# Two conditional residual MLPs in sequence: opening DMAs reordered over two queues, slot tables packed, adapter picks shared between engines

## The reference

```
w1, w2 = W1[language], W2[language]              # 10 languages, 128x32 and 32x128
h = relu(x @ w1 + b1[language])
y = x + h @ w2 + b2[language]
x = x + layernorm(y) * gamma[language] + beta[language]

s0, s1, s2 = relu(x @ share_wi[m]) @ share_wo[m]  # 128 -> 512 -> 128, all sequences
out_a, out_b = the same with experts type and type + 1 of four
e = wa * out_a + wb * out_b                       # weights from softmax(gate_vecs / 0.1)
g = softmax(relu(concat(e[0], s0[0], s1[0], s2[0]) @ gate_w1) @ gate_w2)   # first token
x = x + g0 * e + g1 * s0 + g2 * s1 + g3 * s2
```

## Time and profile before

| | us |
|---|---|
| median of 3 runs | 85.97 (85.92 to 86.11) |
| the profiled execution | 85.84 |
| its span | 83.9 |

### The profile page before, as it was taken

One profiled execution on the slowest core, in us unless ns is written; L12 is line 12 of the kernel. 1 busy time (PEld: TensorE's weight loads), 2 busy tenths in 40 slices (PEclk: granted clock), 3 DMA queues, 4 the chain that ended last, 5 costly groups with the idle time before them and its releaser, 6 DMA issues.

```text
span 83.9 us, 1644 instructions
## 1 busy us (share of the span) xinstructions
PE 77.1 (92%) x458; PEld 64.7 (77%) x458; DVE 56.7 (68%) x161; ACT 54.3 (65%) x136; POOL 44.2 (53%) x92
## 2 busy tenths in 40 slices
PE   4999985999999999999999999999999999999720
PEld 1355645867878899988999988888999998999510
DVE  4357696899659665375445664579749996689930
ACT  0726876595997989997899964745545654566110
POOL 4882452999999877178975400000006981069400
PEclk9999999999999999999999999999999999999999
DMA  0784776899997491000000000000000000210021
GB/s 3 174 174 85 226 208 177 253 299 342 335 286 241 131 324 63 0 0 0 8 0 0 0 0 0 0 4 0 0 8 0 0 0 0 62 62 8 0 71 58
DMA packets 12151, 7.56 MB, mean 90 GB/s; under 512 B 2501, under 2 KB 10969, under 8 KB 12141
## 3 DMA queue, kind: packets, MB, share of 16 engines
q1 hardware_dynamic: 11984, 7.39, 30.7%
q0 software_dynamic: 96, 0.05, 0.6%
q10 hardware_dynamic: 60, 0.01, 0.1%
HBM read 5.87 MB, written 0.52 MB: 76 GB/s over the span
## 4 chain that ended last, share of the span: by engine, by line
PE 75%; DVE 7%; POOL 7%; ACT 4%; issue 3%; DVEq 0%; ACTq 0%
PE bank L1052 10%; PE bank L1003 10%; PE bank L1049 9%; PE bank L1050 9%; PE bank L1004 9%; PE bank L1005 9%; PE bank L1083 4%; POOL prod L530 3%; PE bank L1077 2%; PE bank L1057 2%; PE bank L969 2%; POOL prod L532 2%; PE bank L959 1%; DVE gv L761 1%; PE bank L943 1%
## 5 line engine op out<-in xcount | busy, mean ns | idle before, releaser
L816 DVE SCALAR_TENSOR_TENSOR hl<-bank,hh 128x256 fp32r<-128x256 f32 (+2 forms) x60 | 31.3, 526 | 16.1 <-ACT hh L608 15.7
L608 ACT ACTIVATE hh<-bank 128x256 fp32r<-128x256 f32 (+2 forms) x60 | 28.2, 470 | 14.5 <-PE bank L1005 12.4
L486 POOL TENSOR_TENSOR wl<-w_raw,wh 128x512 fp32r<-128x512 f32 x18 | 23.1, 1290 | 8.5 <-ACT wh L601 8.4
L1052 PE MATMUL bank<-hl,wh 128*128 128x256 f32 (+2 forms) x60 | 20.3, 338 | 0.1
L1049 PE MATMUL bank<-hh,wh 128*128 128x256 f32 (+2 forms) x60 | 19.7, 329 | 0.0
L1050 PE MATMUL bank<-hh,wl 128*128 128x256 f32 (+2 forms) x60 | 19.6, 326 | 0.0
L1052 PEld LDWEIGHTS bank<-hl,wh 128*128 128x128 f32 x60 | 11.3, 189 | 2.1 <-DVE hl L816 1.2
L1049 PEld LDWEIGHTS bank<-hh,wh 128*128 128x128 f32 x60 | 11.4, 190 | 0.9
L1050 PEld LDWEIGHTS bank<-hh,wl 128*128 128x128 f32 x60 | 11.4, 189 | 0.7
L601 ACT ACTIVATE wh<-w_raw 128x512 fp32r<-128x512 f32 x18 | 11.3, 629 | 0.0
L1003 PE MATMUL bank<-x1hl,wh 128*128 128x256 f32 (+1 forms) x34 | 11.2, 329 | 0.0
(11 more groups left out here) (117 smaller groups left out, 111.3 us busy)
## 6 DMA issues: line engine op xcount, KB each, us to landing
w_raw<-in_L_cond_expert_wi_dram SPq DMA_DIRECT2D x6, 256.0 KB, 4.3
w_raw<-in_L_cond_expert_wo_dram SPq DMA_DIRECT2D x6, 256.0 KB, 4.4
w_raw<-in_L_cond_share_wi_dram SPq DMA_DIRECT2D x3, 256.0 KB, 2.9
w_raw<-in_L_cond_share_wo_dram SPq DMA_DIRECT2D x3, 256.0 KB, 3.1
x_in<-in_x_dram SPq DMA_DIRECT2D x2, 256.0 KB, 3.4
xs<-x1hl SPq DMA_DIRECT2D x4, 128.0 KB, 4.5
x1hl<-xs SPq DMA_DIRECT2D x4, 128.0 KB, 2.5
out_dram<-o_sb SPq DMA_DIRECT2D x4, 128.0 KB, 1.9
```

Source lines behind the costliest of these rows:

```text
L486: nc.gpsimd.tensor_tensor(wl[:, k, w, :], w_raw[:, k, buf(w), :], wh[:, k, w, :].bitcast(f32), ALU.subtract).then_inc(s_wl[w], 1)
L608: nc.scalar.activation(packed(hh[:, u % NBUF, :], r), packed(h_ps[u % NBUF][:, :], r), ACT.Relu).then_inc(s_hh, 1)
L816: nc.vector.scalar_tensor_tensor(out=packed(hl[:, u % NBUF, :], r), in0=packed(h_ps[u % NBUF][:, :], r), scalar=0.0, in1=packed(hh[:, u % ...
L1052: nc.tensor.matmul(dst, wh[:, 1, w, chunk], lo, start=False, stop=(c == FC - 1)).then_inc(s_mm2, 1)
```

## The change

- SP's first DMAs are x half 0, W1 and x half 1; `language`, which was ahead of them, and `type`, which was fourth, are issued by ACT: `language` ahead of gamma, beta and b1, `type` behind them.
- WARM goes from 8 to 7.
- Three slot starts or experts are packed in one integer: two tables with 17 memsets in place of six with 24. DVE, not POOL, multiplies, sums and converts. Engines load two integers, and `load_packed` takes three values out of each by shifts and masks.
- POOL takes the four picks of W1 for half 1 in place of ACT.
- On ACT, the copy of xT for half 1 goes ahead of the first root, `weights_high(0, 0)` ahead of the second, and `weights_high(0, 1)` ahead of both x1_high.
- On PE, `transpose_x(1)` goes ahead of `adapter_out(0)`; `load_starts` goes from the end of the opening to a place ahead of `adapter_in(1)`; `adapter_out` is called for each pair, and pairs 2 and 3, which were inside `opening_products`, stand on either side of `transpose_z(1)`.

```diff
-    NQ, NK = 2 * len(SIZES), B + 1
-    STEPS = {0: {3: 3, 4: 3, 5: -3, 6: 3}, 1: {0: 1, 2: 1, 3: -2, 4: 4, 5: 1, 6: -2, 7: 1}, 2: {0: 4, 4: -4},
-             3: {1: -2, 3: 2, 5: -2, 6: 2, 8: -2}, 4: {3: -2, 4: 2, 6: -2}, 5: {4: -2}}
+    NQ, NK = 2, B + 1
+    BITS = (3, 2)
+    STARTS = ({3: 3, 4: 3, 5: -3, 6: 3}, {0: 1, 2: 1, 3: -2, 4: 4, 5: 1, 6: -2, 7: 1}, {0: 4, 4: -4})
+    EXPERTS = ({1: -2, 3: 2, 5: -2, 6: 2, 8: -2}, {3: -2, 4: 2, 6: -2}, {4: -2})
+    STEPS = [{k: sum(at.get(k, 0) << bits * i for i, at in enumerate(what)) for k in range(NK)}
+             for bits, what in zip(BITS, (STARTS, EXPERTS))]
-    WARM = 8
+    WARM = 7
...
+        def load_packed(engine, name, q, tops):
+
+            engine.wait_ge(s_tab, 1)
+            top = (1 << len(SIZES) * BITS[q]) - 1
+            both = loaded(engine, name, tab_i[0:1, B + 2 * q:B + 2 * q + 2], [top] * 2)
+            values = []
+            for (par, i), t in zip(SLOT_OF, tops):
+                reg = engine.alloc_register(f"{name}_{par}{i}")
+                engine.reg_mov(reg, (both[par] >> BITS[q] * i) & ((1 << BITS[q]) - 1))
+                values.append(engine.snap(reg, min_val=0, max_val=t))
+            return values
...
         def _(sp):
-            sp.dma_start(lang_p[:, :], on_all(language)).then_inc(s_lang, 16)
             sp.dma_start(x_in[:, half(0), :], x[half(0), :, :].rearrange("b s d -> s b d")).then_inc(s_x[0], 16)
             sp.dma_start(W1t[:, :, :], W1.rearrange("l d a -> d l a")).then_inc(s_w1, 16)
-            sp.dma_start(kind_p[:, :], on_all(kind)).then_inc(s_kind, 16)
...
-            window_tables()
+            pick_adapters()
+            pool.wait_ge(s_tab, 1)
...
+            act.dma_start(lang_p[:, :], on_all(language)).then_inc(s_lang, 16)
             act.dma_start(par_l[:, 0, :], gamma).then_inc(s_gb, 16)
             act.dma_start(par_l[:, 1, :], beta).then_inc(s_gb, 16)
             act.dma_start(b1_l[:, :], b1).then_inc(s_b1in, 16)
+            act.dma_start(kind_p[:, :], on_all(kind)).then_inc(s_kind, 16)
...
-            pick_adapters(0)
+            pick_adapters()
             add_beta((0, 1))
             adapter_relu(0)
             add_beta((2, 3))
-            pick_adapters(1)
-            standard_deviation(0)
             act.wait_ge(s_xt, 2)
             nc.scalar.activation(xT[:, cols(1)], xt_ps[1][:, :], ACT.Copy).then_inc(s_xtc[1], 1)
+            standard_deviation(0)
+            weights_high(0, 0)
             standard_deviation(1)
-            weights_high(0, 0)
             adapter_relu(1)
+            weights_high(0, 1)
             x1_high(0)
             x1_high(1)
-            weights_high(0, 1)
...
                 stt(key[:, :], kind_f[:, :], float(B), no_b, ALU.mult, ALU.add)
                 tt(sq[:, :, :], across(key[:, :], B), down(key[:, :], B), ALU.is_lt)
-                nc.vector.tensor_reduce(tab[:, 0:B], sq[:, :, :], AX.X, ALU.add).then_inc(s_sorted, 1)
+                total(tab[:, 0:B], sq[:, :, :])
+                dve.wait_ge(s_steps, STEP_COUNT)
+                tt(taken[:, :, :, :], steps[:, :, :, :], reached[:, :, :].unsqueeze(2).to_broadcast([P, 2, NQ, NK]),
+                   ALU.mult)
+                total(tab[:, B:].rearrange("p (q s) -> p s q", s=2), taken[:, :, :, :])
+                nc.vector.tensor_copy(tab_i[:, :], tab[:, :]).then_inc(s_tab, 1)
...
                     with_high(0)
                     if n == 0:
                         with_high(1)
-                        adapter_out(1)
                         pe.wait_ge(s_x1l, 1)
...
             residual(0)
             adapter_in(0)
+            transpose_x(1)
+            adapter_out(0)
             residual(1)
-            adapter_out(0)
-            transpose_x(1)
+            adapter_out(1)
+            starts = load_starts(pe)
+            adapter_in(1)
             residual(2)
-            adapter_in(1)
             transpose_z(0)
             residual(3)
+            adapter_out(2)
             transpose_z(1)
-            starts = load_starts(pe)
+            adapter_out(3)
             opening_products()
```

More of the change, by code:

```diff
@@ L87, in conditional_residual_mlps @@
     BUFS = SH + RING
-    NQ, NK = 2 * len(SIZES), B + 1
-    STEPS = {0: {3: 3, 4: 3, 5: -3, 6: 3}, 1: {0: 1, 2: 1, 3: -2, 4: 4, 5: 1, 6: -2, 7: 1}, 2: {0: 4, 4: -4},
-             3: {1: -2, 3: 2, 5: -2, 6: 2, 8: -2}, 4: {3: -2, 4: 2, 6: -2}, 5: {4: -2}}
+    NQ, NK = 2, B + 1
[4 more added lines that the diff above has]
+             for bits, what in zip(BITS, (STARTS, EXPERTS))]
+    STEP_COUNT = sum(1 for at in STEPS for k, v in at.items() if v and k) + 2 * NQ
+    FIRST_EXPERT = sum(1 << BITS[1] * i for i in range(len(SIZES)))
     UNITS = [(r, c) for r in range(len(RUNS)) for c in range(FC)]
@@ L266, in conditional_residual_mlps @@
         s_steps = sem("s_steps")
-        s_sorted = sem("s_sorted")
         s_tab = sem("s_tab")
@@ L310, in buf @@
             return w if w < SH else SH + (w - SH) % RING
-        def place(k, what):
-            return B + SLOTS * what + k
         def size(k):
@@ L347, in loaded @@
             return [engine.snap(reg, min_val=0, max_val=top) for reg, top in zip(regs, tops)]
+        def load_packed(engine, name, q, tops):
[8 more added lines that the diff above has]
+            return values
         def load_starts(engine):
-            engine.wait_ge(s_tab, 1)
-            return loaded(engine, "start", tab_i[0:1, place(0, 0):place(SLOTS, 0)], [B - size(k) for k in range(SLOTS)])
+            return load_packed(engine, "start", 0, [B - size(k) for k in range(SLOTS)])
         def load_adapters(engine, langs, h):
@@ L392, in _ @@
             load_wo(sp, 1, share_wo[1, :, :])
-            sp.wait_ge(s_tab, 1)
-            experts = loaded(sp, "expert", tab_i[0:1, place(0, 1):place(SLOTS, 1)], [E - 1] * SLOTS)
+            experts = load_packed(sp, "expert", 1, [E - 1] * SLOTS)
             for k in range(RING):
@@ L454, in _, with pick_adapters @@
             link(nc.gpsimd.memset(steps[:, :, :, :], 0.0))
-            for q, at in STEPS.items():
+            for q, at in enumerate(STEPS):
                 for k, v in at.items():
[L457 to L474, removed]
+                    for par in range(2):
+                        value = v + (q * FIRST_EXPERT * (2 + par) if k == 0 else 0)
+                        if value and (par == 0 or k == 0):
+                            pars = slice(par, par + 1) if k == 0 else slice(0, 2)
+                            nc.gpsimd.memset(steps[:, pars, q, k:k + 1], float(value)).then_inc(s_steps, 1)
+            def pick_adapters():
+                pool.wait_ge(s_lang, 16)
+                langs = loaded(pool, "lang", lang_p[0:1, HB:B], [L - 1] * HB)
+                pool.wait_ge(s_w1, 16)
+                for b, lang in zip(range(HB, B), langs):
+                    nc.gpsimd.tensor_copy(W1s[:, b:b + 1, :], W1t[:, bass.ds(lang, 1), :]).then_inc(s_w1c[1], 1)
             def add_beta():
@@ L674, in _ @@
                     ranks.update(zip(range(HB), loaded(act, "rank_", tab_i[0:1, 0:HB], [B - 1] * HB)))
-                    starts = loaded(act, "start", tab_i[0:1, place(0, 0):place(SLOTS, 0)],
-                                    [B - size(k) for k in range(SLOTS)])
+                    starts = load_starts(act)
                 if u == 15:
@@ L960, in residual, with adapter_out @@
                                  stop=False, skip_group_check=True)
-            def adapter_out(h):
-                if h == 0:
+            def adapter_out(n):
+                if n == 0:
                     pe.wait_ge(s_par, 16 * PAIR)
                     pe.wait_ge(s_hot, PAIR)
[L966 to L969, removed]
-                                     start=False, stop=True, skip_group_check=True).then_inc(s_y, 1)
+                pe.wait_ge(s_w2[n], 16 * PAIR)
+                pe.wait_ge(s_h0a, n + 1)
+                nc.tensor.matmul(y_ps[n][:, pair(0)], ha[:, n, :], W2z[:, n, :, :],
+                                 start=False, stop=True, skip_group_check=True).then_inc(s_y, 1)
             def transpose_z(n):
```

11 lines of the change are left out of this document (5 added, 6 removed).

## The result

| | kernel before | changed kernel |
|---|---|---|
| median | 85.94 (85.81 to 86.11, 4 runs) | 88.37 (87.03 to 88.83, 4 runs) |
| the profiled execution | 85.84 | 88.28 |
| its span | 83.9 | 86.4 |

The change makes the kernel slower by 2.1%: the ratio is 1.0213, with a 95% interval of 1.0144 to 1.0282. The forecast was 86.0 with a range to 86.6, so it missed. One sentence is needed on the spread: the four executions of the changed kernel lie 1.8 us apart, and most kernels here, the one before too, have some executions 1 to 4 us longer than the rest, which the comparisons leave out (of the changed kernel they keep 88.28 and 87.03), and in the two of these that were traced (f3 and g2) PE's pace doubles only near 10.4.

A forecast was written before the change was run, and what follows sets the result against it. PE, 92% busy, was taken as the bound, gated by POOL's start at 14.25. Inserted steps losing 0.50 against g's 0.36 gain put that start at 14.26, so 85.97 + 0.0 gives 86.0, range 85.4 to 86.6.

The forecast's parts named there:

- g: How much earlier adapter_out(0) starts than 8.33 on PE: 0.36 us, bounds 0.1 and 0.57.
- the load with its unpacking: PE's load of two integers, 0.3 to 1.0 us, and unpacking of six values, 0.2 to 0.6; covered at middle values.
- the clock: Rival, chance 0.06: one warming product fewer makes PE's pace double later, costing 1.0 us, time 87.0.
- The gate: PE's first_product(4) at 19.23 waits for POOL's low part of set 1, so it moves with POOL's start at 14.25.
- PE's gate isn't POOL: Rival, chance 0.10: PE's shorter opening counts at first_product(4), gaining 0.8 us, time 85.2.
- PE's shorter opening: Moving adapter_out for half 1 and load_starts brings PE to first_product(4) some 0.8 us sooner, only to wait; costed at nothing.
- The two inserted steps: residual(1) between the adapter_out pairs loses 0.24 us, adapter_out(2) ahead of the transposes of z pair 1 loses 0.26.
- PE stays busy until 5.1: At PE's start, the trace argument against a late doubling of its pace after one warming product fewer.
- What else moves: Remaining shifts on DVE, POOL, PE, SP and ACT around the opening, taken as covered or buying nothing.
- the transposes of z come later: Rival, chance 0.24: z pair 1's transposes wait behind adapter_out(2) and PE's load and unpacking; 86.2 to 86.5.
- expert loads: SP's expert loads come 0.4 to 0.7 us sooner, so xs lands sooner, which buys nothing.
- The span stays: The profiled execution's span remains 83.9 us, since POOL's start moves by 0.0.

The follow-up runs named there:

- f3: e4 with eight warming products and PE's load and unpacking of the starts moved ahead of first_product(4); 88.31 us (86.22 to 89.92).
- g2: g1 with residual(1) ahead of adapter_out(0) and adapter_out(2) behind both transposes of z; 85.05 us against 85.84.
- f2: The changed kernel with nine warming products and two more behind the transposes of x; 86.91 us against 85.85 (ratio 1.0122).
- e4: The changed kernel with the opening DMAs on their old queues; 85.95 us against 85.83 (ratio 1.0029).
- g4: f1 with PE's load of the six starts moved ahead of the transposes of z; 85.2 us against 85.84 (ratio 0.9951).
- f5: f3 with residual(1) back ahead of adapter_out(0) and adapter_out(2) back behind transpose_z(1); 86.0 us against 85.85 (ratio 1.0007).
- g3: g2 without POOL's wait for x1_low ahead of the low part of set 0, second half; 85.01 us against 85.84.
- h2: h1 with residual(1) ahead of adapter_out(0) and adapter_out(2) behind transpose_z(1); 85.74 us against 85.76 (ratio 1.0017).
- h1: f2 with PE's load and unpacking of the starts moved behind residual(2); 86.29 us against 85.76 (ratio 1.0079).
- g1: e4 with eight warming products and PE's load and unpacking moved behind adapter_in(1) and residual(2); 85.38 us against 85.84.
- e2: The kernel before with seven warming products in place of eight; 85.66 us against 85.83 (ratio 0.9987).
- e3: The kernel before with only the new queues and order of the opening DMAs; 86.35 us against 85.83 (ratio 1.0076).
- f1: The kernel before with eight added one-element memsets on DVE; 85.15 us against 85.85 (ratio 0.991).
- e1: The changed kernel with eight warming products in place of seven; 86.98 us against 85.83 (ratio 1.0143).

## Why the prediction was wrong, step by step

Three steps failed. The sum had g at 0.36 sooner, the load with its unpacking at nothing and the clock at nothing; in the profiled executions adapter_in(0) came 0.7 later at the upper clock (f2), load and unpacking cost 0.76, and the clock 1.4.

- **The gate.** Right. In each trace PE's shift at first_product(4) is POOL's within 0.05 (3.32 and 3.33; e4 1.0 and 1.02; g4 0.28 and 0.27), unless the load stood there (f3, f5) or POOL's wait was gone (g3). With it the rival "PE's gate isn't POOL" falls, and h2, where PE comes 0.86 sooner through the opening and stands for 0.85, shows that PE's shorter opening is worth nothing. In g3 the gate opened and the second one, at the slot, held the end, as the forecast had it.
- **The two inserted steps.** Right: 0.24 + 0.26 = 0.50 forecast, 0.44 by h1 against h2 (0.57 by g1 against f5, which also takes out the rest of the load).
- **The size of g.** Wrong in sign. I gave x the landing time of its old place, 3.4 after issue. It took 4.1: the chain of the changed kernel has

```profile
0.74 4.12 DMA x_in<-in_x_dram
```

  so it landed at 4.86 and not at 4.14. b1 came later still, behind `language` on ACT's queue; I had allowed at most 0.3 for it and the clock together. adapter_out(0) came at 8.67 where only the queues were changed, so g is -0.34 against a forecast of 0.36 and a lower bound of 0.1. The rule in the Trainium skill that the prediction weighed (DMA: Bandwidth & Descriptors, Issuing engines are not separate DMA queues) has the trace on its side here: x, issued 0.47 sooner, landed at 4.86 and not at 4.61. My error was to treat it as a bound that leaves x where it was, with no price for b1. That `language` is what b1 was behind is my reading only: b1 was also issued 0.5 us later, and x half 1 1.6 us sooner.
- **The clock.** Given 0.06, and it came about, by another way than the one priced. e2 shows that the count of warming products isn't it. "PE stays busy until 5.1" was worked out from the early landing; with x and b1 late, PE stands for 0.64 before 4.99 and works 1.09 of the 1.80 us from 4.36 to 6.16. The price was 1.0; it measured 1.4 (after against f2). So this rival depended on the step before it, and I had treated them as independent.
- **PE's load and unpacking.** The mis-sized term inside "What else moves": 0.3 to 1.0 for the load (0.72, in the range) and 0.2 to 0.6 for unpacking, "by no row". The latter took 1.5. Loading and unpacking take 2.2 to 2.3 together, adapter_in(1) comes at 11.07 in e4 and 11.96 in f2 (12.72 in the changed kernel, where the slow products cover the load), far beyond the 10.0 that the rival "the transposes of z come later" named, and 0.6 to 0.76 of the path is lost. That rival, at 0.24, had this mechanism right; its price, 86.2 to 86.5, was too low. No row of before shows such an instruction on PE, and an unknown cost with no row near it should have kept a wide bound; I capped it at 0.6 and put the cover at 0.3 beside it.
- **SP.** The same term: expert loads were to be 0.4 to 0.7 sooner. They start at 12.45 against 12.53 in the trace of before; the load is 0.48 in place of 1.28, and 1.2 from its end to the first issue (0.3 to 0.4 before) eats the gain. The picks on POOL end near 7.0 and disturb nothing, as forecast.
- **The end.** "The span stays" assumed a fixed end. It became 0.8 us shorter, by an instruction load that fell elsewhere. The DMA view of before shows the packet among the last store, but I hadn't read the instruction queues. This part is luck: no term of the forecast has it. Without that gift the change would have cost 3.3.

The sum with the measured terms, upper clock: late start 0.7 and load and steps 1.2, less 0.8, is 1.1, so 86.9 (f2: 86.92); with the clock's 1.4, 88.3 (88.28). Only the share of x against that of b1 in the late start wasn't separated: no run moved one alone. In h1 and h2 the transposes of x started at 4.76 and 4.79, next to the 4.73 of before, and PE still waited for b1 until 6.18 and 6.38, so there b1 is the larger part. Why x took 4.1 in e3 and in the changed kernel and 3.9 in f2, h1 and h2, with the same queues, stays open.

## What to carry to other kernels

A table packed to shorten a load pays only if what unpacks it is cheap: on PE's sequencer six values cost 1.5 us, more than the 1.0 of loading them all. Issuing a DMA sooner doesn't land it sooner when others are moved up beside it (x left 0.47 sooner and landed 0.25 later), and if PE is the engine that stands for it, it may also lose its clock, so a late start and a slow clock should get one joint chance. Before a fixed end is written into a sum, look whether a block of program is fetched among the last stores: a few idle instructions can be worth more than the edit under study.

## What the runs showed of the hardware

- A packet of an instruction queue (0.01 MB by the view) beside the last store goes with a landing of 2.7 us in place of 1.8 to 1.9 and an end 0.7 to 0.8 us later; eight more instructions on DVE moved it away (f1). The Trainium skill (Runtime: NRT & Kernel Launch, Instruction fetch mechanics) tells that each sequencer fetches its blocks over a DMA queue of its own. The traces agree in that the packets are on queues of their own, q8 and q14 on the page; the cost to another transfer is only in these runs.
- The clock can rise, fall and rise within one opening (e1: up before 4.98, down at 7.60, up at 11.0); ahead of the fall PE had stood for x and b1.
- On PE each unpacked value costs about 1.5 / 6 = 0.25 us of its sequencer, in which no product is issued (e4; an estimate).
- The load of two integers took 0.72 on PE and 0.48 on SP, where eight took 0.54; six took 1.01 on PE and 1.28 on SP before, and POOL's four ranks 0.53 before and 0.33 after. So its length follows neither the count nor the engine alone.
